# Both heads' value products in one step, and a two-tensor scaling on GpSimd

## The reference

```
xn  = layernorm(x)
q, k, v = xn @ Wq + bq, xn @ Wk + bk, xn @ Wv + bv    # 16 heads of 64
att = softmax(causal(q k^T / 8)) / 8
out = x + (att v) @ proj + ffn(xn)
```

## Time and profile before

| | us |
|---|---|
| median of 3 runs | 1488.75 (1488.54 to 1489.19) |
| the profiled execution | 1484.91 |
| its span, first to last instruction | 1482.8 |
| granted TensorE clock, share of full speed | 0.998 |
| TensorE busy | 1433.1 (97%) |
| DVE busy | 1161.3 (78%) |
| ACT busy | 1057.0 (71%) |
| POOL busy | 1351.0 (91%) |

### The profile page before, as it was taken

One profiled execution on the slowest core, in us unless ns is written; L12 is line 12 of the kernel. 1 busy time (PEld: TensorE's weight loads), 2 busy tenths in 40 slices (PEclk: granted clock), 3 DMA queues, 4 the chain that ended last, 5 costly groups with the idle time before them and its releaser, 6 DMA issues. The chain is left out here.

```text
span 1482.8 us, 40863 instructions
## 1 busy us (share of the span) xinstructions
PE 1433.1 (97%) x11036; PEld 1146.4 (77%) x11036; DVE 1161.3 (78%) x4134; ACT 1057.0 (71%) x3032; POOL 1351.0 (91%) x1414
## 2 busy tenths in 40 slices
PE   6999999999999999999999999999999999999998
PEld 5678777777877778778787787878778787777876
DVE  6787878878788787887878778787887878878784
ACT  4777777767777676776777777777777777777774
POOL 5999989999899998999989999998999999999996
PEclk9999999999999999999999999999999999999999
DMA  6444443443444344344443544444444344434431
GB/s 156 106 94 105 101 110 88 103 113 92 105 104 107 90 99 118 88 109 97 107 100 91 123 92 99 104 104 104 91 102 112 92 110 103 107 85 106 108 86 51
DMA packets 112932, 150.65 MB, mean 102 GB/s; under 512 B 18175, under 2 KB 47166, under 8 KB 112830
## 3 DMA queue, kind: packets, MB, share of 16 engines
q1 hardware_dynamic: 112830, 149.68, 42.8%
HBM read 11.20 MB, written 4.19 MB: 10 GB/s over the span
## 5 line engine op out<-in xcount | busy, mean ns | idle before, releaser
L535 POOL TENSOR_SCALAR prob<-prob,rden 128x128 f32<-128x128 f32 (+3 forms) x1024 | 1092.2, 1084 | 81.6 <-DVE rden L798 59.4
L809 DVE CUSTOM_DVE_ANT_0 prob<-scores,mask 128x128 f32<-128x128 f32 (+3 forms) x1024 | 461.6, 485 | 261.3 <-issue 220.1
L613 ACT ACTIVATE prob<-prob,nmax 128x128 f32<-128x128 f32 (+3 forms) x1024 | 564.4, 554 | 102.5 <-DVE nmax L809 99.5
L1060 PE MATMUL ptp<-ident,prob 128*128 128x128 f32 x2560 | 379.3, 275 | 13.7 <-DVE pt L821 9.6
L624 ACT ACTIVATE pt<-ptp 128x128 f32<-128x128 f32 (+3 forms) x512 | 222.1, 434 | 189.7 <-PE ptp L1060 176.5
L1048 PE MATMUL scores<-k_twice,q_parts 128*128 128x128 f32 (+3 forms) x1024 | 332.8, 335 | 17.5 <-DVE nmax L809 9.0
L1084 PE MATMUL zp<-pt,v_sb 128*64 128x64 f32 (+3 forms) x4096 | 335.8, 306 | 0.8 <-DVE z_lo L827 0.8
L1060 PEld LDWEIGHTS ptp<-ident,prob 128*128 128x128 f32 x2560 | 294.8, 140 | 52.0 <-issue 17.6
L1051 PE MATMUL scores<-k_low,q_parts 128*128 128x128 f32 (+3 forms) x1024 | 321.9, 324 | 0.0
L1048 PEld LDWEIGHTS scores<-k_twice,q_parts 128*128 128x128 f32 x1024 | 193.5, 189 | 84.5 <-issue 30.6
L1084 PEld LDWEIGHTS zp<-pt,v_sb 128*64 128x64 f32 x4096 | 210.2, 137 | 53.4 <-issue 43.7
(11 more groups left out here) (141 smaller groups left out, 1703.4 us busy)
## 6 DMA issues: line engine op xcount, KB each, us to landing
k_twice<-k_hi SPq DMA_DIRECT2D x512, 128.0 KB, 2.4
q_parts<-q_hi SPq DMA_DIRECT2D x256, 128.0 KB, 2.4
q_parts<-q_lo SPq DMA_DIRECT2D x256, 128.0 KB, 2.4
xin<-in_L_attn_x_dram SPq DMA_DIRECT2D x16, 256.0 KB, 3.1
xres<-in_L_attn_x_dram SPq DMA_DIRECT2D x16, 256.0 KB, 2.9
out_dram<-osb SPq DMA_DIRECT2D x16, 256.0 KB, 2.5
pt<-in_L_attn_Wq_dram SPq DMA_DIRECT2D x1, 512.0 KB, 4.3
pt<-in_L_attn_Wk_dram SPq DMA_DIRECT2D x1, 512.0 KB, 4.6
```

What stands on the lines that cost most here:

```text
L535: nc.gpsimd.tensor_scalar(part, part, rden[:, s % NROT, h:h + 1], None, ALU.mult)\
L613: nc.scalar.activation(part, part, ACT.Exp, bias=nmax[:, s % NROT, h:h + 1], scale=-1.0, accum_out=den[:, s % NROT, h:h + 1]).then_inc(p_r ...
L809: nc.vector.tensor_tensor_reduce(out=prob[:, s % NROT, h, 0:cols], in0=scores[h][:, 0:cols], in1=mask[:, S - cols:S], scale=-INV_SCALE, sc ...
L1060: done = nc.tensor.transpose(ptp[h][:, P * j:P * j + P], prob[:, s % NROT, h, P * j:P * j + P], ident[:])
```

## The change

`LAG_PV` becomes (9, 9): the value products of head 0 move from the step with i = 0 to the one with i = 1, and stand directly ahead of those of head 1. `normalise` on POOL uses `tensor_tensor` with `rden` repeated along the row as the second tensor in place of `tensor_scalar` with `rden` as a number for each partition. Its wait for the constants falls away, and the count that it waits for is worked out in the wait itself.

```diff
-LAG_PV = (8, 9)
+LAG_PV = (9, 9)
...
             def normalise(c, s):

-                summed = c.fixed(c.unit(s))
-                pool.wait_ge(consts_ready, 3)
-                pool.wait_ge(r_ready, summed)
+                pool.wait_ge(r_ready, c.unit(s))
                 for h in range(2):
                     part = prob[:, s % NROT, h, 0:width(s)]
-                    nc.gpsimd.tensor_scalar(part, part, rden[:, s % NROT, h:h + 1], None, ALU.mult)\
-                        .then_inc(pn_ready, 1)
+                    scale = rden[:, s % NROT, h:h + 1].to_broadcast([P, width(s)])
+                    nc.gpsimd.tensor_tensor(part, part, scale, ALU.mult).then_inc(pn_ready, 1)
```

## The result

The changed kernel takes 1421.35 us (median of 4, 1419.79 to 1421.71) against 1488.64 us (1486.26 to 1489.19): ratio 0.9549, 95% interval 0.9532 to 0.9565, so 4.5% faster. The forecast was faster, 1446, range 1424 to 1480.

What follows compares the result with a forecast made beforehand. TensorE, busy 97%, was taken to bound the kernel, with POOL close behind at 91%. The terms 38 + 18 + 3 - 11 - 5 gave 43 us less, from the median 1488.75 to 1446, range 1424 to 1480.

Steps and rivals of the forecast that it cites:

- denser values: TensorE, second step of each pair: adjacent heads save one entry and exit, 0.30 us a pair, 38 us gained (0 to 46).
- late POOL, steps 12 to 16: TensorE's waits and late transposes behind POOL's queue go: 1.10 us a batch, 18 us gained (10 to 22).
- DVE's heavy stretch, steps 22 to 27: DVE's 1.03 us cast beside POOL's multiply may shrink: 0.2 us a batch, 3 us gained (-8 to 10).
- wait behind the batch boundary: TensorE's scores wait for DVE's late maximum, partly returned at the key DMA: 0.7 x 15, 11 us lost (0 to 18).
- late pairs: Three late pairs of a batch: scores wait for DVE's second maximum, 0.1 us each, 5 us lost (0 to 15).
- What bounds: TensorE, busy 97%, sets the time; gains must come from its waits or denser work; POOL is close at 91%.
- The price on POOL: POOL's scaling as a two-tensor multiply costs 0.66 of before: 1092.2 us become 721, POOL falls to 68%.
- The 704 ns named as a sign: Sign on POOL: the scaling's mean near 704 ns, with POOL busy near 68%.
- One sign did not come: Sign in steps 12 to 16: no wait of DVE for POOL's small power, which was 1.93 us.
- rival B: POOL's two-operand form shuts DVE out: maxima wait 0.35 us each, DVE becomes the bound, about 1550 us; chance 0.06.
- The two halves: Moved values (38 gained, 11 and 5 lost) and POOL's scaling (18 and 3 gained) priced apart, then added: 43 us less.
- case C: More than forecast: 64-wide products gain too, boundary loss hidden, cast shrinks: 73 us less, 1416; chance 0.10.

Runs made afterwards that it cites:

- scaling alone: The changed kernel with LAG_PV back at (8, 9), so only POOL's two-tensor scaling is left of the change: 1442.80 us, ratio 0.9706.
- split: The changed kernel with head 0's values ahead of the second step's transposes and head 1's behind them: 1454.29 us, ratio 0.9785.
- ln22: The kernel before with POOL's layer norm behind the scaling of unit 22 in place of unit 21: 1506.66 us, ratio 1.0142.
- extra_ahead: The changed kernel with one more 128x256 two-tensor multiply of scratch on POOL per batch, ahead of the layer norm: 1431.31 us, ratio 0.9630.
- lag_only: The kernel before with LAG_PV = (9, 9) alone, POOL keeping the one-tensor scaling: 1507.71 us, ratio 1.0149.

## Why the prediction was right in direction and short in size

The terms in us, from the step tables, times 16 (15 for the boundaries), gains positive:

```
term                                         forecast   measured   from
denser values                                   +38        +44     0.34 a pair (0.30 to 0.35)
late POOL, steps 12 to 16                       +18        +22     before - scaling alone: 1.38
DVE's heavy stretch, steps 22 to 27              +3        +17     before - scaling alone: 1.08
wait behind the batch boundary                  -11         -9     steps 0 to 5, less two pairs' 0.34
late pairs                                       -5        -12     steps 24, 25 and 28, 29
```

The size failed at one term above all, the one for DVE's heavy stretch (+3 for +17); the other gains came out 6 and 4 us larger, and a loss that was 7 us larger hid part of that.

- **What bounds.** Right. TensorE stayed at 97%, and the gain came from its waits and from denser work.
- **Denser values.** Right, with the size near the upper bound given. The rows of after show no loss between the heads, and in split 0.29 to 0.31 comes back when they are parted. The Trainium skill, "TensorEngine Tiling (Array Packing)", Key Properties, has it that a change of tiling mode drains the array and another tile of the same mode doesn't; the 0.21 at 682.06 and split agree.
- **The price on POOL.** Right: 0.66 was forecast, 711.9 / 1092.2 = 0.65 measured. (The 704 ns named as a sign was busy time through count; the list's own mean of 1084 gives 1084 x 0.66 = 715, and 722 was measured.) The Trainium skill, "GPSIMD Engine Reference", Elementwise, puts a loop's best case at about 1.8 cycles per element and two inputs at about 2.6. Here the form with one tensor was the slower: 1563 ns at 512 columns against 1041 with two.
- **Late POOL.** Right in place and mechanism, a little small: step 15 gave 0.35 and step 16 0.23, where two rows in them had promised 0.18 and 0.14. One sign did not come: DVE still waits for the small power, 11.2 us in 16 batches after 30.8, without TensorE waiting for it.
- **The DVE stretch: the step that failed most.** The prediction said of the cast at 721.25 "some of the cast's length may go" and "I take 0.2 x 16 = 3 us". In truth all of its excess went, and that of a second instruction in the same stretch: the mechanism was seen, its term was put at +3 us and measured +17. POOL's multiply beside the cast, before, which the earlier trace rows do not show:

```profile
721.09 1.04 POOL L491 TENSOR_TENSOR xn<-xin,meanvar 128x512 f32<-128x512 f32 x1
```

The answers to the earlier trace rows, from the timeline of after, and the two instructions over 16 batches:

```profile
688.32 1.05 POOL L491 TENSOR_TENSOR xn<-xin,meanvar 128x512 f32<-128x512 f32 x1
...
689.25 0.29 DVE L901 CAST gated_parts<-gated 128x256 fp32r<-128x256 f32 x1
...
689.67 0.69 PE L1058 MATMUL ptp<-ident,prob 128*128 128x128 f32 x4
...
690.46 0.19 PEld L971 LDWEIGHTS jobp<-xt_hi,w_hi 128*128 128x128 f32 x1 [0.34 <-DVE osb L831]
690.46 0.50 PE L971 MATMUL jobp<-xt_hi,w_hi 128*128 128x512 f32 x1
```

```profile
L901 DVE CAST gated_parts<-gated x16: 286/288/320, 83.6 to 1381.5; 128x256 fp32r<-128x256 f32 x16
...
L892 DVE TENSOR_TENSOR lg<-lg x16: 170/170/172, 80.2 to 1378.1; 128x16 f32<-128x16 f32 x16
```

Before, the same two had medians of 1033 and 523 ns and least times of 281 and 170:

```profile
L894 DVE TENSOR_TENSOR lg<-lg x16: 170/523/524, 83.4 to 1440.1; 128x16 f32<-128x16 f32 x16
```

(1033 - 288) + (523 - 170) = 1.10 us of DVE time, and the scaling alone took 1.08 from TensorE in steps 23 to 25. The least time was to be had before: the first and the last batch of the trace of before have the cast at 282 and 281 ns. In the last, POOL has no layer norm to do; in the first, the cast began 0.14 us ahead of POOL's multiply. The prediction used one execution of the instruction, saw that POOL was multiplying beside it, and then put a small number where the two ends of the same line gave 0.75.

What stretches the two is POOL's instruction beside them. Over the 14 batches of the loop, medians in us; the last column is the step on TensorE (step 24 holds head 0's values in the kernel before and in ln22, and not in the other two):

```
instruction, run         begins behind    takes    ends behind    step
                         POOL's start              POOL's end
cast, before                 0.16          1.03       0.15        24: 4.31
cast, extra_ahead            0.30          0.89       0.15        24: 3.05
cast, changed kernel         0.94          0.29       0.18        24: 2.45
cast, ln22                   POOL idle     0.28       -           24: 3.55
L894, ln22                   0.07          0.57       0.03        23: 2.97
L894, before                 0.12          0.52       0.03        23: 2.92
L894, lag_only               0.24          0.40       0.03        23: 2.80
L894, scaling alone          POOL idle     0.17       -           23: 2.63
```

POOL's instruction is the 1.04 us multiply L491 beside the cast, and the 0.61 us copy of the keys' low part (L513) beside L894. However early the DVE instruction begins inside it, it ends just behind POOL's end. And TensorE's step follows: in step 23 the four lengths of L894 and the four times of the step come in the same order, and in step 24 the cast's 0.75 (before to ln22) and 0.60 (changed kernel to extra_ahead) are 0.76 and 0.60 of the step.

The stretching did not leave the kernel, it moved. Another small DVE instruction of the router, in step 21, now lies beside POOL's two-tensor scaling; before and after:

```profile
L884 DVE TENSOR_TENSOR lg<-lg,ramp x16: 131/137/457, 79.1 to 1434.4; 128x16 f32<-128x16 f32 x16
```

```profile
L882 DVE TENSOR_TENSOR lg<-lg,ramp x16: 249/952/955, 75.6 to 1373.0; 128x16 f32<-128x16 f32 x16
```

It begins 0.12 us behind the start of a scaling and ends 0.03 behind its end, 0.8 us longer than before, and a second one (L861, step 15) went from 165 to 410 ns. TensorE does not wait for them: steps 20 + 21 take the 5.90 that denser values give. So the mechanism of rival B is real. It misses the maxima, was already in the old kernel in the stretch where TensorE waited for DVE, and in the new kernel lies where DVE has time. That this came out well is in part luck: the prediction said that other two-operand instructions can meet POOL's new form, but not which. Its term for this stretch was -8 to 10; 17 lies outside.

The Trainium skill, "SBUF — State Buffer", Who interferes with whom, says that a DVE instruction with two SBUF inputs contends with a GpSimd instruction that reads SBUF, that a cast can contend too, that one with at most one SBUF input outside DVE's two-port modes does not, and that whoever starts first holds the shared ports for its whole instruction. The table agrees for the cast and for L894, and the maxima, with one operand from PSUM, agree too (485 ns before and after).

- **The batch boundary.** Right in place and size: 9 us lost where 11 were forecast. The timeline of after shows DVE's late maximum and the wait it makes, the answer to the earlier trace rows:

```profile
713.03 0.50 PE L971 MATMUL jobp<-xt_hi,w_hi 128*128 128x512 f32 x1
...
714.34 0.29 DVE L807 CUSTOM_DVE_ANT_0 prob<-scores,mask 128x128 f32<-128x128 f32 x1 [1.36 <-issue]
...
714.69 0.39 PE L1046 MATMUL scores<-k_twice,q_parts 128*128 128x256 f32 x1 [0.69 <-DVE nmax L807]
```

TensorE's idle wait is 0.69 here, 0.53 to 0.83 over the batches, and the DMA wait of the next pair is gone. The traces also bear out that DVE's loop is the cause, which the prediction took without a test. Of the 15 boundaries 13 are turns of the loop: there DVE stands idle for 1.20 to 1.50 us ahead of this maximum, and steps 0 and 1 take 6.21 to 6.51. At the other two, where the list runs from the first batch into the loop and from the loop into the last batch, DVE's idle time is 0 and the two steps take 5.34 and 5.35. What the engine does while it turns is not shown.
- **Late pairs.** The right steps, but a loss of 5 us was forecast and 12 measured, and a wait was left out. The prediction priced only scores that wait for maxima. The values that left the first step had also covered the key job's wait for its bank: in step 24 the job now waits 0.33 us until DVE has read the bank (`osb`, L831, the PEld row at 690.46 above), in step 28 0.20 us (L726), and in step 25 the transposes wait 0.17 us for POOL's scaling. From the four transposes of step 24 to the job it takes 0.79 (689.67 to 690.46), where it is 0.38 at 745.40.
- **The two halves.** The prediction priced them apart and added them. The sum is near the whole only in this order: the scaling gives 43, and with it the move gives 23 (22 forecast). By itself the move loses 22. It was not said that the gain of the move hung on the scaling.
- **Range.** It reached down to 1424 because case C was left at one in ten; the answer was C's kind, 67 us of its 73, but by other terms: 17 for the cast where C had 10, and a boundary loss that was not hidden.

## What to carry to other kernels

A wait that doesn't show may be hidden by the work ahead of it: moving that work away lets it out, so a reordering is priced with the slack of every instruction that moves up, and together with the change that makes the slack. When the same instruction is longer in one iteration than in another, compare its least and its median time over all of them, and look at what the other engine does beside it. Here the difference was the price of that neighbour, and TensorE, which waited at that place, got all of it back when the neighbour moved. The neighbour can then meet another instruction, so look where it goes. Put products of the same array shape next to each other.

## What was not expected of the hardware

A one-tensor multiply on POOL by a number for each partition took 1563 ns for 128x512 in fp32, and the same multiply with that number repeated as a second tensor 1041 ns; at 128 columns 604 and 402. A cast of 128x256 on DVE took 281 to 288 ns where POOL was idle or near its end, and 887 to 1033 ns where it began in the first third of a two-tensor multiply of POOL: it ended 0.15 us behind POOL's end either time. A DVE instruction on 128x16 took 952 ns in place of 137 in the same way. Changing on TensorE from 128x128 products to pairs of 128x64 products and back cost 0.29 to 0.35 us each time, at granted clocks of 0.996 to 0.998, while changing the head within the pairs cost nothing. And a turn of a hardware loop left DVE idle for 1.20 to 1.50 us in the changed kernel.
